# Two attention layers of a decoder: row maxima taken over two PSUM banks at once, exponentials of one head from one bank

## The chip, the core and the metric

The kernel runs on one core of one Trainium2 chip. Its time is the device time of one launch in microseconds (us). Three executions of the kernel before are shown below, with the one that was profiled beside them.

## What is computed

The program is a decoder of twelve layers over an activation of 4 batches x 1024 tokens x 256 features: quantised attention, cross attention, experts, normed attention, a small product, local attention, a state-space layer, another product, a spiking feed-forward layer, linear attention, causal attention, and a retrieval layer. After each comes a residual sum and a layer norm. The change touches two of them, whose reference is, cut to what matters (16 heads of 16 features, sequence length 1024, context length 77):

```python
# normed attention (layer 1, attn)
q = _layernorm((x @ Wq + bq).reshape(b, s, NH, HD), q_scale, q_bias)
k = _layernorm((x @ Wk + bk).reshape(b, s, NH, HD), k_scale, k_bias)
v = _layernorm((x @ Wv + bv).reshape(b, s, NH, HD), v_scale, v_bias)
scores = jnp.einsum('bqhd,bkhd->bhqk', q, k) * HD ** (-0.5)
probs = jax.nn.softmax(scores, axis=-1)
return jnp.einsum('bhqk,bkhd->bqhd', probs, v).reshape(b, s, NH * HD) @ Wo + bo

# causal attention over context and own keys (layer 3, xattn)
q = x @ Wq
k, v = jnp.split(jnp.concatenate((mem, x), axis=1) @ Wkv, 2, axis=-1)
dots = jnp.einsum('bhid,bhjd->bhij', q, k) * scale
dots = jnp.where(j_idx > i_idx + mem_len, -jnp.inf, dots)
out = jnp.einsum('bhij,bhjd->bhid', jax.nn.softmax(dots, axis=-1), v)
return out @ Wout + bout
```

## The kernel before

One function, `split_attention` (L243), builds four of the attention layers (modes "quant", "cross", "normed" and "causal"); the constants that matter are P = 128, GROUP = 512, PACK = 4 heads, HGS = 4 head groups, HALVES = 2, TILES = 8. Queries and keys are split into bf16 parts and stacked on partitions, so that one bf16 matmul gives the exact score of a head. A softmax without overflow needs each query's maximum before its exponential, so each head group is worked through twice.

The **first pass** (steps "max") makes scores with the queries on the partitions: for each of 8 query tiles of 128 and each of 4 heads, a matmul of the query tile against 512 keys into a bank of the tile `ring` (L529, with a masking matmul L532 on the causal diagonal), and a `reduce_max` on VectorE from that bank into `row_max` (L724). Normed has 64 such steps in a head group (2 halves of the keys each); causal has 48, fewer at the early query tiles, and 8 more for the 77 context keys of all four heads (L525, L719). After a group's last maximum the step "turn" reduces and negates the maxima, splits them into three bf16 parts (L728 to L734), turns them with a matmul (L537), copies them out (L739) and sends them through DRAM to the extra rows of `query_stack` (L804, L806), from where the second pass subtracts them inside its matmul.

The **second pass** works in slots. A slot is one tile of 128 keys (or the context), 512 queries (a half) and the four heads of a group. It has the steps ("scores", n, 0), ("scores", n, 1) and, one slot later, ("values", n): a scores step is two matmuls of 512 columns, one a head, into two of the four banks of the tile `scores` (L555, mask L558), and one `exp` of ScalarE over both banks into `probs` (L644); a values step is four fp32 matmuls that accumulate in `outputs` (L575). Normed has 16 slots in a group (8 tiles of keys by 2 halves). Causal has 14 (context and 4 tiles, context and 8 tiles), and those on the diagonal have 384, 256 or 128 columns to a head. After a half's last slot follow "raw" (ScalarE copies `outputs`, L652), "sums" (L583, reciprocal L749) and "normal" (ScalarE L656, matmuls L592, VectorE L753), two and four slots later.

`main_order` (L311) writes the order of the steps, and every engine walks this one list. While group g runs its second pass, the first pass of group g+1 is spread over all but the last three slots: `share` in each, cut into three pieces that stand between the two scores steps (`share[:cuts[0]]`), before the values step and after it. In the groups where queries and keys of another half of the heads are projected (`prepare`: groups 0 and 2 of a batch) the projection's steps stand in the early slots as well, two after each scores step. The last group of the last batch has no maxima beside it. At the start of each layer stands one first pass by itself (`first_order`, for group 0 of batch 0). The batches 0 to 2 are a loop, batch 3 stands alone.

What holds the engines together are counting semaphores on these PSUM tiles. The ring (steps "project", "vproj", "vars", "spread", "max", "turn", "sums", "normal") has two places: step r may be written when step r-2 has been read. The scores tile has two places of two banks: scores step e may be written when exponential e-2 is done.

```python
                            if e >= 2:
                                pe.wait_ge(scores_read if quantised else probs_ready, e - 1)
```

PSUM has 8 banks, all given out here: scores 4, ring 2, outputs 2.

## Time and profile before

| | us |
|---|---|
| median of 3 runs | 12553.13 |
| lowest and highest | 12539.91, 12562.37 |
| the profiled execution | 12566.82 |
| its span in the trace | 12564.9 |
| busy in the span: PE, DVE, ACT, POOL | 9118.7, 6511.5, 4259.1, 2322.7 |
| mean granted TensorE clock, share of 2.4 GHz | 0.818 |

PE is TensorE, PEld its weight loads, DVE VectorE, ACT ScalarE, POOL GpSimd. In a timeline row stand the start from the span's begin, the duration of all that the row merges, engine, line, operation, output<-inputs, shapes, count, and in brackets the idle time of the engine before the row and what ended it. "issue" there means that no wait which the profile shows ended it. Matmuls are pipelined: a row of one matmul lasts longer than the distance to the next. The normed layer's work on attention lies between 2902 and 4370 us, the causal layer's between 9480 and 10610 us.

### The profile page before, as it was taken

The page shows a single profiled execution, that of the slowest core. Times are in us where ns is not written, and L with a number is a line of the kernel's source. Part 1 is how long each engine was busy: PE and PEld are TensorE (multiplying, and loading weights), DVE is VectorE, ACT ScalarE, POOL GpSimd, SP SyncE. Part 2 cuts the span into 40 slices and gives each one's busy share as a digit, 9 for nine tenths or more (in the row PEclk, how much of TensorE's full clock was granted, in tenths as well). Part 3 has the DMA queues.
Part 4 walks back from the last instruction along what each step waited for, and adds up shares of the span by engine and source line. Part 5 has one row for each costly group of instructions (what it writes and reads, how often), then busy time and mean ns, then how long its engine had stood idle before and what let it go on. Part 6 is the DMA issues. An engine that isn't in the chain of part 4 may idle for free. (4 is left out here: it accounts for less than half of the span.)

```text
span 12564.9 us, 119074 instructions
## 1 busy us (share of the span) xinstructions
PE 9118.7 (73%) x41714; PEld 4719.9 (38%) x41826; DVE 6511.5 (52%) x11716; ACT 4259.1 (34%) x6517; POOL 2322.7 (18%) x1916
## 2 busy tenths in 40 slices
PE   4777574975888889888957667677886887454555
PEld 1222243542333356456422222233443443343344
DVE  6666332015556556256258878855344554444443
ACT  3555221112444446255133333322112433232222
POOL 1000002011101011011013323310001000455555
PEclk8888665986999989999978778788777998777777
DMA  3210111112111000000000000000002221568677
GB/s 62 38 32 16 33 31 60 66 57 39 26 22 31 17 11 2 8 11 9 0 11 0 0 0 0 0 9 2 3 0 44 41 32 24 134 142 153 139 148 155
DMA packets 228075, 505.07 MB, mean 40 GB/s; under 512 B 46859, under 2 KB 87669, under 8 KB 226071
## 3 DMA queue, kind: packets, MB, share of 16 engines
q0 software_dynamic: 88064, 282.15, 10.3%
q1 hardware_dynamic: 139527, 216.73, 8.6%
q8 instruction: 273, 4.47, 0.2%
q14 instruction: 211, 1.73, 0.0%
HBM read 426.36 MB, written 75.53 MB: 40 GB/s over the span
## 5 line engine op out<-in xcount | busy, mean ns | idle before, releaser
L644 ACT ACTIVATE probs<-scores 128x1024 f32<-128x1024 f32 (+4 forms) x1024 | 927.4, 941 | 1270.0 <-PE scores L555 974.1
L724 DVE TENSOR_REDUCE row_max<-ring 128x1 f32<-128x512 f32 (+3 forms) x1792 | 1046.5, 628 | 351.0 <-PE ring L529 274.3
L2715 POOL DMA_INDIRECT r_got<-in_L_ffn_tables,r_pick_now x1024 | 988.1, 965 | 674.4 <-issue 288.8
L2803 PE MATMUL r_psum_y<-r_diagonal,r_got 128*128 128x128 f32 x4096 | 611.7, 317 | 522.5 <-ACT r_diagonal L2850 343.2
L555 PE MATMUL scores<-query_stack,key_stack 99*128 99x512 bf16 (+3 forms) x2816 | 856.9, 398 | 140.6 <-DVE levels L746 57.4
L2636 DVE TENSOR_TENSOR_SCAN state<-decay,added 128x1024 f32<-128x1024 f32 x256 | 871.0, 3402 | 35.6 <-ACT decay L2611 31.5
L575 PE MATMUL outputs<-probs,head_values 128*32 128x512 f32 (+3 forms) x5632 | 765.2, 617 | 106.1 <-ACT probs L641 104.2
L2803 PEld LDWEIGHTS r_psum_y<-r_diagonal,r_got 128*128 128x128 f32 x4096 | 589.0, 231 | 579.2 <-ACT r_diagonal L2850 379.7
L529 PE MATMUL ring<-key_stack,query_stack 96*128 96x512 bf16 (+3 forms) x1792 | 642.8, 388 | 151.6 <-DVE row_max L724 59.8
L641 ACT ACTIVATE probs<-levels,quant 128x1024 f32<-128x1024 uint8 x512 | 610.9, 1233 | 388.0 <-DVE levels L746 386.5
L2619 POOL TENSOR_TENSOR added<-ssm_du,state_in_rows 128x1024 f32<-128x1024 f32 x256 | 608.4, 2377 | 592.4 <-DVE state L2636 576.4
L746 DVE TENSOR_SCALAR levels<-scores 128x1024 uint8<-128x1024 f32 x512 | 606.0, 1219 | 135.4 <-PE scores L555 111.3
L2587 PE MATMUL state_sums<-term,constants 128*128 128x512 f32 x1024 | 638.9, 759 | 8.1 <-DVE ssm_u L2627 8.1
L2611 ACT ACTIVATE decay<-ssm_dt,a_log 128x1024 f32<-128x1024 f32 x256 | 294.1, 1149 | 647.5 <-DVE state L2636 647.5
L555 PEld LDWEIGHTS scores<-query_stack,key_stack 99*128 99x128 bf16 x2816 | 261.3, 106 | 624.0 <-DVE levels L746 278.7
L167 ACT ACTIVATE norm_squares<-norm_sum 128x512 f32<-128x512 f32 x208 | 127.6, 630 | 1047.2 <-DVE norm_sum L192 1035.8
L2938 DVE CUSTOM_DVE_ANT_0 r_scratch<-r_got,r_rows_now 128x256 f32<-128x256 f32 x1024 | 378.9, 421 | 191.2 <-DMA r_got<-in_L_ffn_tables,r_pick_now 108.0
L2198 POOL TENSOR_TENSOR norm_squares<-qk,rope 128x256 f32<-128x256 f32 x256 | 180.9, 739 | 1594.0 <-DVE qk L2122 1594.0
L529 PEld LDWEIGHTS ring<-key_stack,query_stack 96*128 96x128 bf16 x1792 | 164.0, 100 | 738.3 <-DVE row_max L724 519.2
L490 PE MATMUL ring<-norm_sum,split_w 128*128 128x512 f32 x448 | 273.4, 755 | 219.8 <-DVE norm_sum L220 128.0
L1929 PE MATMUL window_products<-wide_w,shifted 128*128 128x512 f32 x768 | 365.2, 627 | 57.9 <-DVE shifted L2099 49.3
L2572 PE MATMUL state_out<-ssm_states,pick 96*128 96x512 bf16 x512 | 169.6, 416 | 309.2 <-DVE term L2641 308.3
(512 smaller groups left out, 16197.9 us busy)
## 6 DMA issues: line engine op xcount, KB each, us to landing
expert_w<-in_L_ffn_w SPq DMA_DIRECT2D x16, 1024.0 KB, 10.4
r_got<-in_L_ffn_tables,r_pick_now POOLq DMA_INDIRECT x1024
quant_parts<-parts SPq DMA_DIRECT2D x48, 256.0 KB, 5.5
query_stack<-quant_parts SPq DMA_DIRECT2D x48, 256.0 KB, 8.3
key_stack<-quant_parts SPq DMA_DIRECT2D x48, 256.0 KB, 8.7
query_stack<-cross_parts SPq DMA_DIRECT2D x48, 256.0 KB, 8.2
normed_parts<-parts SPq DMA_DIRECT2D x48, 256.0 KB, 4.9
query_stack<-normed_parts SPq DMA_DIRECT2D x48, 256.0 KB, 8.4
```

The costliest lines, as they stand in the source:

```text
L529: last = nc.tensor.matmul(out[:, 0:cols], lhs, k_stack[0:max_row, h, j * GROUP:j * GROUP + cols], start=True, stop=not edge)
L555: last = nc.tensor.matmul(out[:, off:GROUP], keys, q_stack[0:rows, h, half * GROUP + off:(half + 1) * GROUP], start=True, stop=not edge)
L575: last = nc.tensor.matmul(o_ps[SLOT * i:SLOT * (i + 1), half, off:GROUP], vals, probs[0:k_rows, n % 2, i // 2, i % 2, off:GROUP], start=fi ...
L641: nc.scalar.activation(dst, levels[:, e % 2, :, :], ACT.Exp, bias=quant[:, 4:5], scale=scale).then_inc(probs_ready, 1)
L644: nc.scalar.activation(dst, s_ps[0:k_rows, 2 * (e % 2):2 * (e % 2) + 2, off:GROUP], ACT.Exp, scale=scale).then_inc(probs_ready, 1)
L724: nc.vector.reduce_max(row_max[:, i, qt, at:at + 1], src[:, 0:cols], AX.X).then_inc(ring_read, 1)
L746: ts(levels[:, e % 2, :, :], s_ps[:, 2 * (e % 2):2 * (e % 2) + 2, :], 0.0, QMAX, ALU.max, ALU.min).then_inc(scores_read, 1)
L2587: last = nc.tensor.matmul(sum_ps[:, half(j)], chip.c(C_ID), term[:, i % 2, half(j)], start=(n == 0), stop=(n == STATES - 1))
L2619: nc.gpsimd.tensor_tensor(added[:, i % 2, :], du[:, i // STATES, :], state_in[:, i % 2, :], ALU.mult).then_inc(added_ready, 1)
L2636: nc.vector.tensor_tensor_scan(state[:, i % 2, :], decay[:, i % 2, :], added[:, i % 2, :], 0.0, ALU.mult, ALU.add).then_inc(state_ready, 1)
L2715: nc.gpsimd.indirect_dma_start(out=b["got"][:, n, :], out_offset=None, in_=b["tables"], in_offset=bass.IndirectOffsetOnAxis(ap=b["pick_now ...
L2803: last = nc.tensor.matmul(y_ps[:, c, t * P:(t + 1) * P], row, b["diagonal"][:, k % 2, n, :], start=False, stop=(k == RHEADS * per - 1 and ...
```

## The change

In the modes normed and causal a maximum step now covers all keys of a query tile: one or two matmuls into the two banks of one ring place, and one `reduce_max` over up to 1024 elements. The ring has still two places, now of two banks each (4 banks). The scores tile has two banks, each a place for one head: after each score matmul stands its own semaphore step, and ScalarE does one exponential for each head from one bank. Modes quant and cross are as before. Core of the diff:

```diff
@@ -260,7 +260,9 @@
     blocks = [(t, m) for m in range(2) for t in range(sides)]
-    kinds = (1 if context else 0) + (HALVES if own else 0)
+    kinds = (1 if context else 0) + (1 if own else 0)
+    score_heads = 1 if maxed and own else 2
+    ring_banks = 2 if maxed and own else 1
 
...
@@ -282,7 +284,7 @@
             if own:
-                out += [(qt, i, j) for i in range(PACK) for j in range(1 + qt // PER_HALF if causal else HALVES)]
+                out += [(qt, i, (qt + 1) * P if causal else SEQ) for i in range(PACK)]
         return out
...
@@ -513,10 +515,11 @@
                         elif kind == "max":
-                            _, g, nx, qt, i, j = step_
+                            _, g, nx, qt, i, cols = step_
                             if step_[3:] == first_pass(g)[0]:
                                 stacks_ready(g, nx)
                             out = ring_bank(step_)
+                            both = r_ps[:, ring[step_] % 2, :, :].rearrange("p j t -> p (j t)")
                             heads = range(PACK) if i is None else [i]
...
@@ -524,12 +527,12 @@
                                 else:
-                                    cols = min(GROUP, (qt + 1) * P - j * GROUP) if causal else GROUP
-                                    edge = causal and j == qt // PER_HALF
-                                    last = nc.tensor.matmul(out[:, 0:cols], lhs, k_stack[0:max_row, h, j * GROUP:j * GROUP + cols],
-                                                            start=True, stop=not edge)
-                                    if edge:
-                                        last = nc.tensor.matmul(out[:, cols - P:cols], chip.id_bf[:, :], chip.far_n[:, :], start=False, stop=True)
+                                    for at in range(0, cols, GROUP):
+                                        end = min(at + GROUP, cols)
+                                        edge = causal and end == cols
+                                        last = nc.tensor.matmul(both[:, at:end], lhs, k_stack[0:max_row, h, at:end], start=True, stop=not edge)
+                                        if edge:
+                                            last = nc.tensor.matmul(both[:, cols - P:cols], chip.id_bf[:, :], chip.far_n[:, :], start=False, stop=True)
                             last.then_inc(ring_ready, 1)
...
@@ -539,30 +542,31 @@
                             g, half, kt, off = slots[n]
-                            e = 2 * n + pair
                             if n % per_group == 0 and pair == 0:
                                 stacks_ready(g, 0)
                                 if ("turn", g, 0) in turns:
                                     pe.wait_ge(top_loaded, 16 * (turns[("turn", g, 0)] + 1))
-                            if e >= 2:
-                                pe.wait_ge(scores_read if quantised else probs_ready, e - 1)
                             for i in range(2):
+                                e = (4 * n + 2 * pair + i) // score_heads
+                                if e >= 2 and i % score_heads == 0:
+                                    pe.wait_ge(scores_read if quantised else probs_ready, e - 1)
                                 h = PACK * g + 2 * pair + i
                                 k_rows = CTX if kt is None else P
                                 keys = keys_now[0:rows, h, :] if kt is None else k_stack[0:rows, h, kt * P:(kt + 1) * P]
-                                out = s_ps[0:k_rows, 2 * (e % 2) + i, :]
+                                out = s_ps[0:k_rows, score_heads * (e % 2) + i % score_heads, :]
                                 edge = diagonal(half, kt)
                                 last = nc.tensor.matmul(out[:, off:GROUP], keys, q_stack[0:rows, h, half * GROUP + off:(half + 1) * GROUP],
                                                         start=True, stop=not edge)
                                 if edge:
                                     last = nc.tensor.matmul(out[:, off:off + P], chip.id_bf[:, :], chip.far_t[:, :], start=False, stop=True)
-                            last.then_inc(scores_ready, 1)
+                                if i % score_heads == score_heads - 1:
+                                    last.then_inc(scores_ready, 1)
                         elif kind == "values":
                             n = step_[1]
                             g, half, kt, off = slots[n]
                             k_rows = CTX if kt is None else P
                             first, final = (kt, off) == items(half)[0], (kt, off) == items(half)[-1]
-                            pe.wait_ge(probs_ready, 2 * n + 2)
+                            pe.wait_ge(probs_ready, PACK // score_heads * (n + 1))
                             if own and n == old_slots:
...
@@ -631,18 +635,21 @@
                             g, half, kt, off = slots[n]
-                            e = 2 * n + pair
                             k_rows = CTX if kt is None else P
                             if n >= 2:
                                 act.wait_ge(outputs_added, n - 1)
                             dst = probs[0:k_rows, n % 2, pair, :, off:GROUP]
                             if quantised:
+                                e = 2 * n + pair
                                 act.wait_ge(scores_read, e + 1)
                                 nc.scalar.activation(dst, levels[:, e % 2, :, :], ACT.Exp, bias=quant[:, 4:5], scale=scale).then_inc(probs_ready, 1)
                             else:
-                                act.wait_ge(scores_ready, e + 1)
-                                nc.scalar.activation(dst, s_ps[0:k_rows, 2 * (e % 2):2 * (e % 2) + 2, off:GROUP], ACT.Exp,
-                                                     scale=scale).then_inc(probs_ready, 1)
+                                for i in range(0, 2, score_heads):
+                                    e = (4 * n + 2 * pair + i) // score_heads
+                                    bank = score_heads * (e % 2)
+                                    act.wait_ge(scores_ready, e + 1)
+                                    nc.scalar.activation(dst[:, i:i + score_heads, :], s_ps[0:k_rows, bank:bank + score_heads, off:GROUP], ACT.Exp,
+                                                         scale=scale).then_inc(probs_ready, 1)
                         elif kind == "raw":
...
@@ -714,14 +721,13 @@
                         elif kind == "max":
-                            _, g, nx, qt, i, j = step_
+                            _, g, nx, qt, i, cols = step_
                             if i is None:
                                 nc.vector.reduce_max(row_max[:, :, qt, 0], src[:, 0:PACK * CTX].rearrange("p (i n) -> p i n", i=PACK),
                                                      AX.X).then_inc(ring_read, 1)
                             else:
-                                cols = min(GROUP, (qt + 1) * P - j * GROUP) if causal else GROUP
-                                at = j + kinds - HALVES
-                                nc.vector.reduce_max(row_max[:, i, qt, at:at + 1], src[:, 0:cols], AX.X).then_inc(ring_read, 1)
+                                both = r_ps[:, r % 2, :, :].rearrange("p j t -> p (j t)")
+                                nc.vector.reduce_max(row_max[:, i, qt, kinds - 1:kinds], both[:, 0:cols], AX.X).then_inc(ring_read, 1)
                         elif kind == "turn":
...
@@ -813,7 +819,7 @@
         def batch(order, b, b_next):
-            with banks(nc, "scores", [P, 4, GROUP], F32) as s_ps, banks(nc, "ring", [P, 2, GROUP], F32) as r_ps, \
+            with banks(nc, "scores", [P, 2 * score_heads, GROUP], F32) as s_ps, banks(nc, "ring", [P, 2, ring_banks, GROUP], F32) as r_ps, \
                     banks(nc, "outputs", [P, 2, GROUP], F32) as o_ps:
                 attend(order, b, b_next, s_ps, r_ps, o_ps)
             if b is not None:

```

The hunks left out give the new counts to the other waits (`PACK // score_heads * old_slots` on `scores_ready`, and `r_ps[:, r % 2, 0, :]` for the ring steps of one bank).

What it does to the order of instructions, at two places. TensorE, normed layer, two slots of a group with maxima, before (L529 is a maximum's matmul, L555 a score's, L575 a value's):

```order
L555 MATMUL scores<-query_stack,key_stack 128x512 x2
L529 MATMUL ring<-key_stack,query_stack 128x512
L555 MATMUL scores<-query_stack,key_stack 128x512 x2
L529 MATMUL ring<-key_stack,query_stack 128x512 x2
L575 MATMUL outputs<-probs,head_values 32x512 x4
L529 MATMUL ring<-key_stack,query_stack 128x512 x2
L555 MATMUL scores<-query_stack,key_stack 128x512 x2
L529 MATMUL ring<-key_stack,query_stack 128x512
L555 MATMUL scores<-query_stack,key_stack 128x512 x2
L529 MATMUL ring<-key_stack,query_stack 128x512 x2
L575 MATMUL outputs<-probs,head_values 32x512 x4
L529 MATMUL ring<-key_stack,query_stack 128x512 x2
```

and the same place of the changed kernel (L533, L558 and L579 are those lines now):

```order
L558 MATMUL scores<-query_stack,key_stack 128x512 x4
L533 MATMUL ring<-key_stack,query_stack 128x512 x2
L579 MATMUL outputs<-probs,head_values 32x512 x4
L533 MATMUL ring<-key_stack,query_stack 128x512 x4
L558 MATMUL scores<-query_stack,key_stack 128x512 x4
L533 MATMUL ring<-key_stack,query_stack 128x512 x2
L579 MATMUL outputs<-probs,head_values 32x512 x4
L533 MATMUL ring<-key_stack,query_stack 128x512 x2
```

Between the first and the second pair of score matmuls stood one maximum; now all four score matmuls of a slot follow each other, since `len(share) // 5` is 0 for shares of two, three or four. A maximum is a row of x2 now: the first slot shown has one before its values and two behind them, the second has one and one.

ScalarE, normed layer, from the first slots after the projections on, before (L644 is the exponential):

```order
L644 ACTIVATE probs<-scores 128x1024 x8
L652 ACTIVATE raw_out<-outputs 128x512
L644 ACTIVATE probs<-scores 128x1024 x6
L656 ACTIVATE wide_inverse<-inverse 128x512
L644 ACTIVATE probs<-scores 128x1024 x10
L652 ACTIVATE raw_out<-outputs 128x512
L644 ACTIVATE probs<-scores 128x1024 x6
```

and now (L651):

```order
L651 ACTIVATE probs<-scores 128x512 x16
L659 ACTIVATE raw_out<-outputs 128x512
L651 ACTIVATE probs<-scores 128x512 x12
L663 ACTIVATE wide_inverse<-inverse 128x512
L651 ACTIVATE probs<-scores 128x512 x20
L659 ACTIVATE raw_out<-outputs 128x512
L651 ACTIVATE probs<-scores 128x512 x12
```

Each exponential became two of half the size; nothing else moved on ScalarE.

In slots without maxima TensorE's rows read alike before and now (four score matmuls, four values matmuls). What differs there is that the third and the fourth score matmul now wait for the exponentials of the first and the second head of their own slot, where before they waited for the slot before.

## Rows read from the trace of the kernel before

**Rows 1.** Page, part 5: shapes, count, busy us, mean ns, idle us.

```profile
L644 ACT ACTIVATE probs<-scores 128x1024 f32<-128x1024 f32 (+4 forms) x1024 | 927.4, 941 | 1270.0 <-PE scores L555 974.1
L724 DVE TENSOR_REDUCE row_max<-ring 128x1 f32<-128x512 f32 (+3 forms) x1792 | 1046.5, 628 | 351.0 <-PE ring L529 274.3
```

**Rows 2.** Stretches of the normed stage, first line naming the columns.

```profile
core 0: us, PE busy (x) PEld busy (x) DVE busy (x) ACT busy (x) POOL busy (x), PEclk, DMA share, GB/s
2970.00:3015.00 45.00, 37.74 (x63) 6.44 (x63) 39.94 (x62) 0.00 (x0) 0.00 (x0) 0.50 0.00 0
3290.00:3590.00 300.00, 249.92 (x1236) 100.45 (x1228) 174.28 (x295) 131.96 (x143) 23.81 (x14) 0.92 0.10 17
4290.00:4335.00 45.00, 40.76 (x254) 10.96 (x246) 1.89 (x4) 36.66 (x41) 0.00 (x0) 1.00 0.01 2
```

**Rows 3.** Timeline, one normed slot with maxima: start us, us, instruction.

```profile
3446.65 3.11 DVE L724 TENSOR_REDUCE row_max<-ring 128x1 f32<-128x512 f32 x5 [0.57 <-PE ring L529]
3446.66 0.60 PE L555 MATMUL scores<-query_stack,key_stack 99*128 99x512 bf16 x2
3447.36 1.98 ACT L644 ACTIVATE probs<-scores 128x1024 f32<-128x1024 f32 x2 [0.40 <-PE scores L555]
...
3447.39 0.39 PE L529 MATMUL ring<-key_stack,query_stack 96*128 96x512 bf16 x1
...
3448.91 1.06 PE L575 MATMUL outputs<-probs,head_values 128*32 128x512 f32 x8
```

**Rows 4.** ScalarE's timeline, normed: where a group with maxima begins and ends.

```profile
3116.08 1.94 ACT L644 ACTIVATE probs<-scores 128x1024 f32<-128x1024 f32 x2 [1.97 <-PE scores L555]
...
3177.22 1.94 ACT L644 ACTIVATE probs<-scores 128x1024 f32<-128x1024 f32 x2 [0.38 <-PE scores L555]
```

**Rows 5.** Timeline, normed, the last batch's last group, without maxima.

```profile
4293.60 1.94 ACT L644 ACTIVATE probs<-scores 128x1024 f32<-128x1024 f32 x2 [0.33 <-PE scores L555]
...
4313.14 0.11 PEld L555 LDWEIGHTS scores<-query_stack,key_stack 99*128 99x128 bf16 x2 [0.32 <-ACT probs L644]
...
4313.68 1.06 PE L575 MATMUL outputs<-probs,head_values 128*32 128x512 f32 x8
...
4314.68 1.34 PE L555 MATMUL scores<-query_stack,key_stack 99*128 99x512 bf16 x4
...
4316.94 1.06 PE L583 MATMUL ring<-constants,raw_out 128*128 128x4 f32 x8
...
4334.09 0.60 ACT L652 ACTIVATE raw_out<-outputs 128x512 f32<-128x512 f32 x1 [1.19 <-PE outputs L575]
```

**Rows 6.** Groups by shape, causal stage, 9540 to 10590 us.

```profile
L724 DVE TENSOR_REDUCE row_max<-ring 128x1 f32<-128x512 f32 x384 | 255.3, 687 | 67.5 <-PE ring L529 46.7 <-PE ring L532 12.9
...
L644 ACT ACTIVATE probs<-scores 128x512 f32<-128x512 f32 x64 | 36.4, 596 | 91.4 <-PE scores L558 91.4
```

**Rows 7.** Groups by shape, normed stage, 2960 to 4340 us.

```profile
L652 ACT ACTIVATE raw_out<-outputs 128x512 f32<-128x512 f32 x32 | 19.1, 598 | 17.0 <-PE outputs L575 17.0
...
L699 DVE TENSOR_REDUCE value_root<-norm_squares 128x64 f32<-128x1024 f32 x7 | 8.5, 1210 | 0.0
```

**Rows 8.** Timeline, normed, after a group's last maximum.

```profile
3107.76 0.22 DVE L728 TENSOR_REDUCE top<-row_max 128x32 f32<-128x64 f32 x1
...
3109.44 0.23 PE L537 MATMUL ring<-identity_bf,top_parts 128*96 128x128 bf16 x1 [0.96 <-DVE top_parts L731]
...
3115.38 1.04 PE L555 MATMUL scores<-query_stack,key_stack 99*128 99x512 bf16 x4 [1.58 <-DMA query_stack<-normed_top]
```

**Rows 9.** ScalarE's timeline, causal: a group with maxima, and the last one.

```profile
9654.48 1.93 ACT L644 ACTIVATE probs<-scores 77x1024 f32<-77x1024 f32 x2 [2.31 <-PE scores L555]
...
9706.97 1.93 ACT L644 ACTIVATE probs<-scores 77x1024 f32<-77x1024 f32 x2 [3.54 <-PE scores L555]
...
10552.24 1.93 ACT L644 ACTIVATE probs<-scores 77x1024 f32<-77x1024 f32 x2 [2.27 <-PE scores L555]
...
10584.62 0.66 ACT L644 ACTIVATE probs<-scores 128x256 f32<-128x256 f32 x2 [0.37 <-PE scores L558]
```

10 lines of the change are left out of this document (5 added, 5 removed).

## The prediction

> **What bounds the kernel now.** I read the page's groups first, then the stretches of the two layers, then single slots in the timeline. The page's groups [rows 1] give the two instructions that the change merges and splits: 1792 reductions of VectorE with a mean of 628 ns and 1024 exponentials of ScalarE with a mean of 941 ns. Of these 1024 the change leaves 64 of cross attention alone. No engine is full in these layers: in 300 us of the normed layer [rows 2] PE is busy 250 us by a count that overstates it, DVE 174, ACT 132. So the time is made by hand-offs between engines, and one slot has to be read in the timeline.
>
> In a slot with maxima [rows 3] DVE works 3.11 us on five reductions and idles 0.57 us, so such a slot lasts 3.68 us. PE has four score matmuls, five of maxima and four values matmuls. A row of two 512-column matmuls lasts 0.60 us where one alone lasts 0.39, so they follow each other at 0.21; nine make 1.9 us. The values matmuls hold PE for 1.00 us, from 4313.68 to the next score matmul at 4314.68 [rows 5]. That is 3.0 us of PE in 3.68. The rest is mostly PE waiting for a place in the ring. ACT, with two exponentials in 1.98 us, idles for the rest. A whole group of 16 slots lasts 61.1 us, 3116.08 to 3177.22 [rows 4].
>
> Three hand-off times come from the same rows. Score matmul to exponential: the pair starts at 3446.66, its second matmul 0.21 later, the exponential at 3447.36, so 0.48 from a matmul's start to its reader's. Reader to matmul: the first reduction starts at 3446.65 and lasts 0.68, the matmul it lets go starts at 3447.39, so 0.06. Last score matmul to the values: 4313.14 plus 0.21 to 4313.68 [rows 5], 0.32.
>
> **VectorE's part.** 512 pairs of reductions in the normed layer and 256 in the causal one (query tiles 4 to 7 of 4 groups, 4 heads, 4 batches) become one each. A reduction of 512 elements takes 687 ns from PSUM [rows 6]; one of 1024 takes 1210 ns from SBUF [rows 7]. None of 1024 from two banks is in this trace: it lies between 1210 and 2 x 687 = 1374 ns. I take 1210, since only the source differs. Five reductions follow each other at (3.11 - 0.68) / 4 = 0.61 us, so a merged one follows at about 1.15: a pair saves 0.07 to 0.16 us of DVE. Where DVE alone sets the pace this is the whole gain. The first pass that stands alone is such a place: 62 reductions in 45 us with the clock at 0.50 [rows 2], some 0.70 each with the hand-off. 64 of them are 44.8 us, 32 merged ones at 1.23 are 39.4: 5 us less, and 2 less in the causal layer.
>
> A rule of the Trainium skill speaks here. "VectorE: DVE Perf Modes", in its section on the TRN2 errata, gives 120 cycles at 0.96 GHz as fixed for a PSUM source, paid once for each instruction. By that a merged pair saves 0.125 us, and if DVE's instruction cost decided everywhere the 768 pairs would give 96 us. The trace agrees with the size but not with the use: DVE idles 0.57 us in each slot [rows 3].
>
> **ScalarE's part, and the wait it adds.** 960 exponentials become 1920. One of 512 elements (two heads of 256) takes 596 ns [rows 6]; a copy of one full bank takes 598 [rows 7], so I take 0.60 for one head and 0.50 from start to start (two of 1.02 take 1.94 to 1.98, so they overlap by about 0.1). ACT has room for that. What counts is the place for the result. Before, scores place e waited for exponential e-2, which was a pair of the slot before, long done. Now it is a head of the same slot, so the third score matmul waits for the first head's exponential and the fourth for the second's. From the first exponential's start of a full slot: the second starts at 0.50 and ends at 1.10, the fourth matmul starts at 1.16, the values 0.32 later at 1.48, they hold PE to 2.48, and the next slot's first exponential starts 0.48 after that, at 2.96. Behind the waiting matmul everything of PE is queued: values, maxima, sums.
>
> The bounds of this slot: 2.48 if the second exponential's end cost nothing (0.48 shorter), 3.2 if a hand-off costs twice what it does here. I take 2.96, because each piece has a row. The slot without maxima lasts 2.12 us before: from 4293.60 to 4334.09 a group lasts 40.5 us [rows 5], of which the sums and normals of two halves take some 6.
>
> *Normed, last group of the last batch.* 16 x 2.96 + 5 for sums, normals and raw copies is 52.5 against 40.5: **+12**.
>
> *Normed, groups with maxima and no projection.* A maximum is two matmuls, 0.43 us of PE, 32 of them in a group. 16 x 2.96 = 47.4; 13.8 for maxima; two sums and two normals at some 0.9 each (eight passes in 1.06 [rows 5]) 3.7; the turn 1.0, since its chain of 1.7 us on DVE (3107.76 to 3109.44 [rows 8]) starts a reduction later; 0.3 for a raw copy. Sum 66.2, against 61.1 [rows 4]. Ring places come in time: with three maxima to a slot DVE has 3.5 us of work in 4.2, and the place of each is read before PE needs it. Eight such groups: 8 x 5.0 = **+40**. The transfer of the maxima (5.9 us from the turn to the next group's first matmul [rows 8]) now lies under two longer slots and costs nothing more.
>
> *Normed, groups with projections.* Seven groups. In slots 1 to 6 the projection's steps stand between the two score pairs and cover the wait, and DVE's saving counts there, some 0.3 a slot. The ten other slots lose as above, less what sums and normals win when DVE is not the one waited for: some +3. Together +1.4 each, **+10**.
>
> *Causal.* A group lasts 52.5 us, 9654.48 to 9706.97 [rows 9]; the others of this kind average 51.5. Eight of 14 slots are full ones at 2.96 (3.05 for the masked ones); 384, 256 and 128 columns give 2.5, 1.9 and 1.6 by the same sum. That is 35.7 for the group. Maxima take 12 of PE, sums and normals 3.7, the turn 1.4, the transfer behind it 1.3 (two narrow last slots do not cover 5.9), and about 1 goes to places in the ring, where four wide maxima stand in one slot. Sum 55: +3.5, eight times, **+28**. With projections I take +2.5, seven times, **+17**. The last group (32.4 us, 10552.24 to 10584.62 [rows 9]) goes to 39.5, **+7**.
>
> *Sum.* Normed 12 + 40 + 10 - 5 = +57, causal 28 + 17 + 7 - 2 = +50, together +107 us. The profiled execution, 12566.8, becomes 12674. It lies 13.7 above the median of the runs, so against that median I predict **12660**. Quant and cross attention keep their code and their time. SP and POOL queues keep their steps; their waits on scores come at the same slot.
>
> **Rivals.** A difference within 0.2%, 25 us, is about what a measurement cannot tell from none.
>
> *DVE sets the pace (faster, 0.14).* PE waits for ring places in every slot with maxima before, and if the new wait for ACT falls wholly into that old one, a slot goes with DVE: 2.46 reductions at 1.15 plus the old 0.57 of idleness is 3.40, against 3.68. With 13 such slots in 15 groups that is -55, half as much in the causal layer, -7 for the first passes, and +19 for the last groups: about -70, **12480**. For it: DVE is what PE is seen waiting for [rows 1]. Against: four scores without a maximum between them put 0.7 us of waiting where PE has nothing else. The point from which it decides is that wait: under about 0.35 us a slot the kernel is faster.
>
> *The two cancel (0.11).* If the ring's stalls in the groups with projections and in the causal layer shrink by 3 us more in each group than I count, 22 groups give back 66, and the time is 12590 or less, down to 12560.
>
> *The clock falls (slower, 0.15).* The lone first pass, where PE waits in every step, was granted 0.50 (1.2 GHz), the last group, where PE hardly waits, 1.00 (2.4 GHz) [rows 2]. If the slots without maxima, PE working 1.9 us in 2.96, or others fall to 1.2 GHz, such a slot takes matmuls of 0.43 and values of 2.0 and lasts some 4.4. A slot with maxima gains about 3. The layers have 256 + 224 = 480 slots; one in twenty at half clock is +72, one in ten +144, on top of the forecast: **12730** to 12800. "TensorE: Matmul & The Clock Gate", Part 1, says that the throttled state is the default and that activity releases it. This rule speaks against the change, which thins PE's work. Against this rival: slots at 3.0 in 3.68 us run at 0.92.
>
> **How the numbers follow.** Forecast 0.60 (12600 to 12740, from 2 us less to 2.5 more in each of 30 groups), the rivals 0.14, 0.11 and 0.15. Slower is 0.60 + 0.15 = 0.75, same 0.11, faster 0.14. The range leaves out half of the faster case and the clock's far end: 12530 to 12770; the forecast's own is 12600 to 12740.
>
> **What would show it.** Exponentials of one head at 0.60 and reductions at 1.2 us. Normed slots without maxima at 2.96 and with them at 3.8 and 4.2. PE's score matmuls waiting for the exponential, some 0.7 us a slot, where they hardly waited before, and PE's waits for `row_max` mostly gone. A normed group of 66 us. I would be wrong if score matmuls three and four start without a wait, if full slots with maxima stay below 3.7, or if the granted clock falls clearly.

## The result, and the profile after

The change makes the kernel slower.

| | before | after |
|---|---|---|
| median of 4 runs, us | 12557.75 | 12754.08 |
| lowest and highest | 12539.91, 12592.83 | 12750.59, 12759.7 |
| ratio, 95% interval | | 1.0153 [1.0131, 1.0176] |
| span in the trace | 12564.9 | 12748.8 |
| busy: PE, DVE, ACT | 9118.7, 6511.5, 4259.1 | 9201.2, 6455.6, 4357.7 |

That is +196 us between the medians and +184 between the traces, where +107 was predicted. The lines below are those of part 5 of the page of after that answer to [rows 1], with the score matmuls beside them (L558 for L555).

```profile
L651 ACT ACTIVATE probs<-scores 128x512 f32<-128x512 f32 (+5 forms) x1984 | 1023.8, 566 | 1338.2 <-PE scores L558 970.5
L730 DVE TENSOR_REDUCE row_max<-ring 128x1 f32<-128x1024 f32 (+7 forms) x1024 | 986.2, 988 | 568.2 <-PE ring L533 347.3
L558 PE MATMUL scores<-query_stack,key_stack 99*128 99x512 bf16 (+3 forms) x2816 | 944.0, 405 | 355.1 <-ACT probs L651 200.7
```

VectorE has 60 us less to do in its maxima (1046.5 to 986.2) and idles 217 more before them; ScalarE has 96 us more in its exponentials. TensorE's line is the one to read: 201 us of its score matmuls' idle time end with an exponential. The view of waits says it for both halves of the engine (columns: us in total, times, longest). Before:

```profile
PEld ring L529 <- DVE row_max L724: 519.2, 878, 1.7
...
PE ring L529 <- DVE row_max L724: 59.8, 226, 1.3
PEld scores L555 <- ACT probs L644: 57.1, 85, 1.6
```

After:

```profile
PEld scores L558 <- ACT probs L651: 601.3, 887, 2.6
PE scores L558 <- ACT probs L651: 217.5, 438, 2.1
...
PEld ring L533 <- DVE row_max L730: 173.9, 244, 1.7
```

The wait for a ring place (579 us by these two lines before, 195 after) has given way to a wait for the exponential (57 before, 819 after). PEld and PE overlap, so these are no parts of the time, but the exchange is plain.

One normed slot without maxima, of the last group, in the timeline of after (it answers to [rows 5]):

```profile
4369.45 2.22 ACT L651 ACTIVATE probs<-scores 128x512 f32<-128x512 f32 x4 [0.72 <-PE scores L558]
4370.09 0.10 PEld L558 LDWEIGHTS scores<-query_stack,key_stack 99*128 99x128 bf16 x1 [1.02 <-ACT probs L651]
4370.10 0.88 PE L558 MATMUL scores<-query_stack,key_stack 99*128 99x512 bf16 x2 [0.53 <-ACT probs L651]
4370.58 0.10 PEld L558 LDWEIGHTS scores<-query_stack,key_stack 99*128 99x128 bf16 x1 [0.39 <-ACT probs L651]
4370.90 0.16 PEld L579 LDWEIGHTS outputs<-probs,head_values 128*32 128x32 f32 x8 [0.23 <-issue]
4370.91 1.06 PE L579 MATMUL outputs<-probs,head_values 128*32 128x512 f32 x8
```

The third score matmul starts 0.65 after the first exponential's start, the fourth 0.48 later, the values at 1.46. The prediction had 1.16 for the fourth and 1.48 for the values.

Where the time went is read from the starts of each group's first exponential. Normed, a group with maxima (it answers to [rows 4]; the last slots before its end stand too):

```profile
3120.57 2.22 ACT L651 ACTIVATE probs<-scores 128x512 f32<-128x512 f32 x4 [0.72 <-PE scores L558]
...
3180.17 2.22 ACT L651 ACTIVATE probs<-scores 128x512 f32<-128x512 f32 x4 [1.65 <-PE scores L558]
3183.12 2.22 ACT L651 ACTIVATE probs<-scores 128x512 f32<-128x512 f32 x4 [0.72 <-PE scores L558]
3186.06 2.22 ACT L651 ACTIVATE probs<-scores 128x512 f32<-128x512 f32 x4 [0.72 <-PE scores L558]
```

65.5 us, where it was 61.1. Causal, a group with maxima (it answers to [rows 9]), with its five slots from the first full one of the second half on, between 10025.03 and 10053.30:

```profile
10003.26 2.23 ACT L651 ACTIVATE probs<-scores 77x512 f32<-77x512 f32 x4 [0.83 <-PE scores L558]
...
10025.03 2.22 ACT L651 ACTIVATE probs<-scores 128x512 f32<-128x512 f32 x4 [0.41 <-PE scores L558]
10031.24 1.09 ACT L651 ACTIVATE probs<-scores 128x512 f32<-128x512 f32 x2 [3.99 <-PE scores L558]
10032.59 1.09 ACT L651 ACTIVATE probs<-scores 128x512 f32<-128x512 f32 x2 [0.27 <-PE scores L558]
10037.73 2.22 ACT L651 ACTIVATE probs<-scores 128x512 f32<-128x512 f32 x4 [4.05 <-PE scores L558]
...
10042.94 2.22 ACT L651 ACTIVATE probs<-scores 128x512 f32<-128x512 f32 x4 [2.47 <-PE scores L558]
10047.78 2.28 ACT L651 ACTIVATE probs<-scores 128x512 f32<-128x512 f32 x4 [2.62 <-PE scores L561]
10053.30 0.87 ACT L651 ACTIVATE probs<-scores 128x384 f32<-128x384 f32 x2 [3.23 <-PE scores L561]
...
10062.25 2.23 ACT L651 ACTIVATE probs<-scores 77x512 f32<-77x512 f32 x4 [2.21 <-PE scores L558]
```

59.0 us for the group, and 28.3 for the five slots. The same group of before lasts from 9917.27 to 9969.60, 52.3 us, and its five slots 22.3:

```profile
9939.18 1.94 ACT L644 ACTIVATE probs<-scores 128x1024 f32<-128x1024 f32 x2 [0.62 <-PE scores L555]
...
9961.52 1.51 ACT L644 ACTIVATE probs<-scores 128x768 f32<-128x768 f32 x2 [2.66 <-PE scores L558]
```

By kind of group, each length being the distance between two such starts (the last group: to its last exponential) and the first pass counted from its first reduction to the first exponential, the layers split so. "Seven" are the groups with projections, "eight" the others with maxima.

| us | first pass | seven | eight | last | sum |
|---|---|---|---|---|---|
| normed, before | 52.9 | 653.5 | 615.3 | 38.3 | 1360.0 |
| normed, after | 46.2 | 651.3 | 653.0 | 51.8 | 1402.3 |
| normed, predicted change | -5 | +10 | +40 | +12 | +57 |
| normed, measured | -7 | -2 | +38 | +14 | **+42** |
| causal, before | 44.3 | 439.4 | 521.9 | 32.7 | 1038.3 |
| causal, after | 40.3 | 492.9 | 594.4 | 45.7 | 1173.3 |
| causal, predicted change | -2 | +17 | +28 | +7 | +50 |
| causal, measured | -4 | +54 | +73 | +13 | **+135** |

42 and 135 make 177 of the 184 us between the traces. The normed layer did what was forecast; the causal one lost almost three times as much. The stretches of the causal layer, from its first exponential to its last, show the clock (columns as in [rows 2]). Before:

```profile
9590.00:10586.00 996.00, 870.03 (x5991) 412.36 (x5989) 531.91 (x1106) 421.77 (x543) 90.34 (x63) 0.93 0.22 36
```

After, and below it the slot that begins at 10031.24:

```profile
9633.00:10766.00 1133.00, 950.01 (x5973) 415.62 (x5974) 505.34 (x866) 466.00 (x989) 90.28 (x62) 0.89 0.19 31
...
10030.00:10037.00 7.00, 6.68 (x30) 2.26 (x30) 2.19 (x5) 2.17 (x4) 0.00 (x0) 0.53 0.00 0
```

Since the granted clock has two levels, 1.2 and 2.4 GHz, a stretch of L us granted c has spent 2 (1 - c) L at the lower one: some 139 us before and 249 after, each uncertain by about 11 through the rounding of c. The normed layer was granted 0.92 before (3024.9 to 4332) and 0.93 after (3028.2 to 4384): there this time did not grow.

### The profile page after: what moved, and what is told of

The parts are those of the page before. It is cut to its first block and busy times, and to the rows that moved or that the text cites. A ratio compares the mean times of both kernels' runs of the same rounds, so it can differ in the third digit from the quotient of the medians.

```text
span 12748.8 us, 119266 instructions
## 1 busy us (share of the span) xinstructions
PE 9201.2 (72%) x41714; PEld 4712.1 (37%) x41826; DVE 6455.6 (51%) x10948; ACT 4357.7 (34%) x7477; POOL 2321.7 (18%) x1916
## 5 line engine op out<-in xcount | busy, mean ns | idle before, releaser
L651 ACT ACTIVATE probs<-scores 128x512 f32<-128x512 f32 (+5 forms) x1984 | 1023.8, 566 | 1338.2 <-PE scores L558 970.5
L730 DVE TENSOR_REDUCE row_max<-ring 128x1 f32<-128x1024 f32 (+7 forms) x1024 | 986.2, 988 | 568.2 <-PE ring L533 347.3
L558 PE MATMUL scores<-query_stack,key_stack 99*128 99x512 bf16 (+3 forms) x2816 | 944.0, 405 | 355.1 <-ACT probs L651 200.7
L579 PE MATMUL outputs<-probs,head_values 128*32 128x512 f32 (+3 forms) x5632 | 779.7, 629 | 104.9 <-ACT probs L645 104.5
L558 PEld LDWEIGHTS scores<-query_stack,key_stack 99*128 99x128 bf16 x2816 | 262.2, 105 | 1068.1 <-ACT probs L651 555.6
L533 PE MATMUL ring<-key_stack,query_stack 96*128 96x512 bf16 (+3 forms) x1792 | 541.9, 389 | 75.6 <-DMA key_stack<-normed_parts 36.7
L2259 PE MATMUL gated_psum<-norm_sum,gated_w 128*128 128x512 f32 x768 | 347.1, 615 | 6.9 <-DVE norm_sum L2306 6.9
```

Of the source, the lines that this page charges most:

```text
L533: last = nc.tensor.matmul(both[:, at:end], lhs, k_stack[0:max_row, h, at:end], start=True, stop=not edge)
L558: last = nc.tensor.matmul(out[:, off:GROUP], keys, q_stack[0:rows, h, half * GROUP + off:(half + 1) * GROUP], start=True, stop=not edge)
L579: last = nc.tensor.matmul(o_ps[SLOT * i:SLOT * (i + 1), half, off:GROUP], vals, probs[0:k_rows, n % 2, i // 2, i % 2, off:GROUP], start=fi ...
L651: nc.scalar.activation(dst[:, i:i + score_heads, :], s_ps[0:k_rows, bank:bank + score_heads, off:GROUP], ACT.Exp, scale=scale).then_inc(pr ...
L730: nc.vector.reduce_max(row_max[:, i, qt, kinds - 1:kinds], both[:, 0:cols], AX.X).then_inc(ring_read, 1)
```

## The experiments

The kernel before was measured anew beside each group of runs. Its median is 12562.25 us beside the first four runs below, 12337.34 beside the next four, 12343.78 beside balanced, warm and three_job_balanced, and 12354.67 beside balanced_warm. So each ratio stands against the before that was measured beside it, and medians in us are not to be compared across these groups. The 200 us between them lie behind the two layers: from the causal layer's last exponential to the end of the trace it is 1980 to 2011 us in before, after and the first four runs, and 1768 to 1780 in the others; why is not known. The layers' own times can be compared over all runs: code that was equal gave 1305.9 and 1307.0 us for the normed layer of before and 1348.2 to 1356.0 for that of after (first exponential to last, as all layer times below). The layers' differences add up to 5 to 35 us less than those of the medians. Repeats of equal code in the causal layer lie up to 9 us apart, and less than that is read as nothing here.

### One layer at a time

The function of before stands beside that of after, and one of the two layers calls it:

```diff
-        split_attention(chip, "causal", params)
+        split_attention_old(chip, "causal", params)
```

(normed_only; causal_only does it for "normed".)

> The change in the normed layer alone, the causal layer as before. In the two traces the normed layer's first pass went from 52.9 to 46.2 us and its main part from 1307 to 1356, so +42 us over before if the layers are independent: about 12600. If part of the loss lies elsewhere (other layers, another clock state), it would be over +60 or under +25.

Measured: 12622.0, ratio 1.0044 [1.003, 1.0059]; normed 1348.2 (before 1307.0), causal 985.4 (994.0). That is 60 us between the medians for the 42 expected, at the edge of what the expectation allowed; the normed layer itself, with its first pass, is 35 us longer.

> The change in the causal layer alone. Traces: first pass 44.2 to 40.3 us, main part 994 to 1133, so +135 us, about 12690. The hand-off sum of the prediction gave +50 for it. The rival (what is missing is not the causal layer's own, but a chance of the profiled execution's clock) expects +50 to +80.

Measured: 12715.38, ratio 1.0124 [1.0108, 1.0141]; normed 1305.9, causal 1128.8, near the expectation. The two excesses, 0.44% and 1.24%, add up to 1.68% against the 1.53% of the whole change: within the intervals the layers do not touch each other, and most of the loss is the causal layer's.

### The exponentials alone, with two places and with four

Both keep the maxima and the ring of before and give each head its exponential. One has two places of one bank for scores, as the change has; the other four, which is all of the four banks that before uses.

```diff
+    score_heads = 1 if maxed and own else 2
+    places = 2 if maxed and own else 2
...
                             for i in range(2):
+                                e = (4 * n + 2 * pair + i) // score_heads
+                                if e >= places and i % score_heads == 0:
+                                    pe.wait_ge(scores_read if quantised else probs_ready, e - places + 1)
```

(exp_only_4: `places = 4 if maxed and own else 2`.)

> Exponentials of one head, two places of one bank, maxima as before (ring of two single banks). Place theory: PE has the waits of the changed kernel and in addition the old waits for ring places, with DVE's work per slot at 3.1 us instead of 2.8: the same as the changed kernel or up to 120 us slower, 12750 to 12870. If the merged maxima are what costs, this is close to before, under 12620.

Measured: 12738.76, ratio 1.0138 [1.0121, 1.0155]; normed 1381.9, causal 1082.6.

> As the last, but with four places of one bank (the four banks that the scores had before). Place theory: the fourth matmul again waits only for a head of the slot before, so the time is that of before within 40 us, though ScalarE does 1920 exponentials instead of 960. Instruction theory (the count of exponentials and of their semaphore steps costs): about as slow as the changed kernel, over 12680.

Measured: 12567.77, ratio 1.0004 [0.999, 1.0018]; normed 1309.5, causal 989.4. This pair is the core of the study: the first came out just under its expectation (12750 or more), the second as expected. The same 1984 exponentials, in the pages' part 5, first with two places:

```profile
L650 ACT ACTIVATE probs<-scores 128x512 f32<-128x512 f32 (+5 forms) x1984 | 1025.5, 567 | 1309.3 <-PE scores L557 963.2
...
L557 PE MATMUL scores<-query_stack,key_stack 99*128 99x512 bf16 (+3 forms) x2816 | 931.8, 400 | 266.0 <-ACT probs L650 110.5
```

and with four:

```profile
L650 ACT ACTIVATE probs<-scores 128x512 f32<-128x512 f32 (+5 forms) x1984 | 982.3, 574 | 1195.2 <-PE scores L557 917.6
...
L557 PE MATMUL scores<-query_stack,key_stack 99*128 99x512 bf16 (+3 forms) x2816 | 849.2, 396 | 138.1 <-DVE levels L752 55.2
```

The view of waits shows the mechanism itself. TensorE's waits for an exponential, with two places:

```profile
PEld scores L557 <- ACT probs L650: 454.5, 870, 2.1
...
PE scores L557 <- ACT probs L650: 116.7, 285, 1.4
```

and with four, where they are back at the 57 us of before:

```profile
PEld scores L557 <- ACT probs L650: 49.9, 95, 0.8
```

960 more instructions on ScalarE cost nothing that can be measured; what costs is that two heads of scores can be under way and not four. Halving the places alone (exp_only_2 against exp_only_4) makes +72 us in the normed layer and +93 in the causal one; against before it is +75 and +89. Merging the maxima as well (after against exp_only_2) gives back 26 us in the normed layer (and 7 in its first pass), and costs 50 more in the causal one (1133.0 against 1082.6). Single groups say the same: the second group of each batch lasts in the causal layer 51.5 us on average before, 57.0 with two places, 59.7 after; the five slots above last 22.3, 25.2 (10030.60 to 10055.80) and 28.3. So the causal loss has two parts, the places and the merging, and the second is looked at further below.

### Three places

The changed kernel with a third place for scores. Its bank comes from `outputs`, which gets one bank; the first values matmul of a half then waits for the raw copy of the half before.

```diff
+    places, out_banks = (3, 1) if maxed and own else (2, 2)
...
-                                if e >= 2 and i % score_heads == 0:
-                                    pe.wait_ge(scores_read if quantised else probs_ready, e - 1)
+                                if e >= places and i % score_heads == 0:
+                                    pe.wait_ge(scores_read if quantised else probs_ready, e - places + 1)
...
-                            if first and g:
-                                pe.wait_ge(raw_ready, HALVES * (g - 1) + half + 1)
+                            made = HALVES * g + half
+                            if first and made >= out_banks:
+                                pe.wait_ge(raw_ready, made - out_banks + 1)
```

> The changed kernel with a third scores place, its bank taken from outputs (one bank instead of two, each half's first values waits for the copy of the half before). Place theory: the third matmul waits for nothing, the fourth for the first head; a full slot without maxima goes from 2.96 to about 2.46 us, 0.5 us a slot over 480 slots: some -200 us from the changed kernel, 12550 or below. Clock theory (the causal layer's loss is the clock): in the causal layer alone more than half of the gain. Instruction theory: no gain, 12750.

Measured: 12380.09, ratio 1.0037 [1.0024, 1.005]; normed 1277.1, which is 30 us below before, causal 1052.4. By the ratios that is some 145 us less than after, where 200 were expected. ScalarE's timeline in the last normed group:

```profile
4255.79 2.07 ACT L653 ACTIVATE probs<-scores 128x512 f32<-128x512 f32 x4 [0.39 <-PE scores L559]
4258.25 2.06 ACT L653 ACTIVATE probs<-scores 128x512 f32<-128x512 f32 x4 [0.39 <-PE scores L559]
```

A slot is 2.46 us with three places, 2.94 with two: 0.48 less, and near the 2.48 that the prediction had as the lower bound of a slot. One bank moved takes back about three quarters of the loss, and turns the normed layer's sign: with the wait shortened, it is faster than before. That this is the gain of the merged maxima is likely but not shown, for no run has three places without them.

### Work between the score matmuls

Two ways to fill the wait without a bank. In the first the values step of the slot before stands between the two pairs of score matmuls, and the second piece of the slot's maxima with it (values_between; values_before is the same move in the kernel before, as a control). In the second one maximum of each slot does (job_between).

```diff
+            early = own and maxed
...
-            order.append(("scores", n, 1))
-            order += maxima(target, nx, share[cuts[0]:cuts[1]])
+            if not early:
+                order.append(("scores", n, 1))
+                order += maxima(target, nx, share[cuts[0]:cuts[1]])
             if n:
...
+            if early:
+                order += maxima(target, nx, share[cuts[0]:cuts[1]])
+                order.append(("scores", n, 1))
```

```diff
-            cuts = [len(share) // 5, 3 * len(share) // 5]
+            cuts = [min(1, len(share)) if own and maxed else len(share) // 5, max(1, 3 * len(share) // 5)]
```

> The changed kernel with the values step moved between the two score pairs, so that PE has 1.0 us of work where it waits for exponentials. Place theory: a full slot without maxima 2.96 to 2.67 us, with maxima PE is free of the wait and DVE's 2.8 us decides, 4.0 to about 3.2: -200 to -350 us, 12400 to 12550, below before. If the waits are not what costs, nothing changes (12750).

Measured: 12405.1, ratio 1.0051 [1.0035, 1.0068]; normed 1311.4, causal 1050.3. By the ratios some 125 us less than after; 200 to 350 were expected, and a time below before.

> The same move in the kernel before. PE hardly waits for exponentials there, DVE's 3.1 us a slot stays: -50 to +30 us, so 12510 to 12590. If the move by itself is worth as much as in the changed kernel (rival: it smooths the ring's use), -150 or more.

Measured: 12420.77, ratio 1.0059 [1.0043, 1.0076]; normed 1353.2, causal 1005.5. That is +83 us, where -50 to +30 were expected. The move slows the kernel before, which has the wait hardly at all: it is no gain in itself. Most of the loss sits in the normed groups with maxima alone (615.3 to 642.5 us) and in the last one (38.3 to 53.0).

> The changed kernel with one maximum of every slot moved between the score pairs. It fills 0.43 us of the wait of some 0.7: 0.4 us in 13 of 16 normed and 11 of 14 causal slots of 15 groups each, 360 x 0.4 = -140 us from the changed kernel, about 12610. If the wait is not filled by it, or the ring stalls in its place, under -50.

Measured: 12414.98, ratio 1.0065 [1.0049, 1.0082]; normed 1311.5, causal 1066.0. By the ratios some 110 us less than after, where 140 were expected. Against the spans of the unchanged code given above (1348.2 to 1356.0, and 1128.8 to 1133.0) both moves give back 37 to 45 us in the normed layer and 63 to 83 in the causal one. The waits tell the same: TensorE's waits for an exponential, 819 us in after, are 287 in values_between and 474 in job_between, where the waits for a ring place grew from 195 to 416. Two different fillers gain where this wait shrinks, which supports that the wait itself is what is paid for.

### The late causal slots: the share, and the clock

What makes the second half of the causal miss? `main_order` deals out the maxima of a group by count, over 11 slots. Before there were 56 of them, none wider than 512; now there are 40, and the 16 that cover over 512 columns, two matmuls and a masking matmul each, all belong to the late query tiles and fall into the late slots. Where the time lies is read from the starts of the exponentials, added up over the fifteen causal groups with maxima. "Late" are the five slots marked out above, "first" the six before them, "end" the last three slots with the way to the next group:

| us | first | late | end | last group | sum |
|---|---|---|---|---|---|
| before | 417 | 319 | 225 | 33 | 994 |
| exp_only_2 | 446 | 363 | 229 | 45 | 1083 |
| after | 433 | 416 | 238 | 46 | 1133 |
| balanced (below) | 448 | 376 | 244 | 46 | 1114 |

The late slots alone make 97 of the layer's 139 us, and the whole of what merging adds (53 for 50, the other parts nearly cancel). One late slot of after in the timeline:

```profile
10028.53 0.11 PEld L533 LDWEIGHTS ring<-key_stack,query_stack 96*128 96x128 bf16 x2
10028.54 0.45 PE L533 MATMUL ring<-key_stack,query_stack 96*128 96x512 bf16 x2
10028.69 1.56 DVE L730 TENSOR_REDUCE row_max<-ring 128x1 f32<-128x640 f32 x2 [0.21 <-PE ring L535]
...
10029.57 1.13 PE L587 MATMUL ring<-constants,raw_out 128*128 128x4 f32 x8 [0.52 <-DVE row_max L730]
...
10030.55 1.02 PE L558 MATMUL scores<-query_stack,key_stack 99*128 99x512 bf16 x2
...
10031.89 1.10 PE L558 MATMUL scores<-query_stack,key_stack 99*128 99x512 bf16 x2 [0.32 <-ACT probs L651]
...
10033.92 1.93 PE L579 MATMUL outputs<-probs,head_values 128*32 128x512 f32 x8
```

The sums at 10029.57 wait 0.52 us for a ring place behind two wide reductions. From about 10030.4 on the matmuls run at the lower clock level (a row of two 1.02 where it was 0.60, the values 1.93 where they were 1.06), and the slot whose first exponential starts at 10031.24 lasts 6.49 us, to 10037.73. TensorE had waited several times in the microseconds before that: for this ring place, and for the exponentials of its own slot. Three runs try to separate the share and the clock. `balanced` deals by columns, a maximum over 512 counting twice; `warm` puts a spare matmul, overwritten by the one behind it, ahead of the second score matmul of a slot; `balanced_warm` has both.

```diff
+            if causal and jobs:
+                weights = [2 if job[2] and job[2] > GROUP else 1 for job in jobs]
+                starts = [sum(weights[:k]) for k in range(len(jobs))]
+                share = [job for job, at in zip(jobs, starts) if s < spread and sum(weights) * s // spread <= at < sum(weights) * (s + 1) // spread]
```

```diff
+                                if causal and i and not pair:
+                                    nc.tensor.matmul(out[:, 0:GROUP], keys, q_stack[0:rows, h, half * GROUP:(half + 1) * GROUP], start=True, stop=True)
```

> The changed kernel; in the causal layer alone a slot's share of maxima is counted in keys' halves (a merged maximum of over 512 keys counts two) instead of in steps, so that the wide ones do not all fall into the last five slots of the share. The causal layer's main part was 1133 us in the changed kernel, 1083 with the same exponentials and unmerged maxima. Share theory: the 50 us between are the uneven share, so 1085 to 1100, and the ratio to before falls from 1.015 to about 1.012. Rival (the two-bank reduction itself, or the ring's coarser places, cost them): within 15 us of 1133.

Measured: 12503.37, ratio 1.0141 [1.0119, 1.0162]; causal 1113.9, granted 0.89 as in after. Expected were 1085 to 1100 if the share were all of the 50 us, and within 15 of 1133 if it were nothing; it lies between.

> The changed kernel; in the causal layer every slot's second score matmul is preceded by a spare matmul of 512 columns into the same place, overwritten by the real one, in a stretch where TensorE waits for an exponential anyway (slack 0.29 us in a full slot, spare 0.22; narrow slots pay some 0.1 to 0.2, 6 of 14, +12 us in the layer). Clock theory: part of the causal layer's loss is the granted clock, which in the changed kernel is 1.2 GHz for 76 us in slot 7 of the groups, against 18 before: the low-clock time of the layer falls from 239 us to under 190 and the main part from 1133 to 1110 or below. Rival (low clock there costs nothing, since other engines are waited for): the low-clock time falls, the time rises by 0 to 15 us.

Measured: 12508.93, ratio 1.0135 [1.0118, 1.0152]; causal 1117.9, granted 0.91, so some 201 us at the lower level. Both went the expected way and less far (under 190 us and 1110 or below were expected).

> Both last single changes in the changed kernel: the causal share counted in halves of keys, and the spare matmul where TensorE waits. Each alone took 19 and 15 us from the causal layer's main part (1133). If share and clock are two separate causes: 1095 to 1105, low-clock time under 200 us, close to the 1083 of the kernel with unmerged maxima, and what is left of the 50 us would be the ring's coarser places. If the two act on the same slots (the low clock of slot 7 is itself made by the share): 1110 to 1118.

Measured: 12505.86, ratio 1.0124 [1.0107, 1.0142]; causal 1103.2, granted 0.91; 1095 to 1105 was expected for two separate causes. The ratios' intervals overlap that of after, so the reading rests on the layer's own time: 1133.0 and 1128.8 for the unchanged code, 15 to 19 us less with the even share, 11 to 15 less with the spare matmuls, 26 to 30 less with both. The even share left the granted clock where it was and took 40 us out of the late slots, of which 15 came back in the first slots and 6 at the end: this part is shown. The spare matmuls' gain lies only just above the 9 us by which equal code differs, and it is spread evenly (5 us in the first slots, 5 in the late ones, 4 at the end), so it is indicated and no more. That the two gains add up in the third run speaks for two separate causes. Together they account for about half of the 50 us that merging costs in this layer; the other 20 to 25 stay open. After the even share what is left against exp_only_2 lies in the late slots (13 us) and at the groups' ends (15).

### All that helped, together

Three places, one maximum between the pairs and the even share:

> Three places for scores (one bank of outputs), one maximum of each slot between the score pairs, and the share of the causal maxima counted in halves of keys. Sums from the single runs: normed main part 1277 (three places), less 0.43 in 13 of 16 slots of eight groups and less in the others, about 1225; causal 1052, less 30 for the share and 20 for the job between, about 1000; first passes 11 us shorter than before. Against before 1307 and 994: -80 us, ratio 0.993. If DVE decides normed slots at 3.2 us (its work is 2.8), normed stays at 1250: ratio 0.996.

Measured: 12299.75 against 12343.78 for before, ratio 0.9961 [0.9946, 0.9975]; normed 1267.0, causal 986.0. It is the one version that is faster than before, if only by 0.4% where 0.7% was expected: -40 us in the normed layer, -6 and -4 in the first passes, and the causal layer level with before (-8, within the 9 us of equal code). The causal layer in it:

```profile
9520.50:10506.50 986.00, 872.52 (x5974) 413.68 (x5976) 506.98 (x866) 451.57 (x989) 90.28 (x62) 0.91 0.22 36
```

against the same window of balanced_warm, with two places:

```profile
9623.60:10726.80 1103.20, 973.07 (x6201) 433.13 (x6203) 510.41 (x866) 475.61 (x989) 90.31 (x62) 0.91 0.20 32
```

The granted clock is the same, the length is not: here the places and the filled wait decide, not the clock.

## Why the prediction was right in kind and too small in size

**VectorE's part: right.** A reduction over 1024 columns of two banks takes 1222 ns (482 of them in the normed layer), for the 1210 taken, so a pair costs 2 x 687 - 1222 = 152 ns less; the first passes became 7 and 4 us shorter, for 5 and 2. "VectorE: DVE Perf Modes" in the Trainium skill, section on the TRN2 errata, gives 120 cycles, 0.125 us, as fixed for each instruction with a PSUM source; the measured saving is somewhat larger. As the prediction held against the rule, it buys nothing by itself: merging gave back 26 us in the normed layer and cost 50 in the causal one. (62 reductions in 45 us [rows 2] are 0.73 us each and not "some 0.70"; the first pass's gain is a difference and hardly moves by it.)

**ScalarE's part: right.** One head takes 595 ns, for 0.60. A full slot without maxima lasts 2.94 us, for 2.96. The chain "third matmul waits for the first head's exponential" is in the rows, and exp_only_4 shows that the exponentials cost nothing besides it: with four places the loss is gone.

**Normed: right, with one term too large.** Slots with two and three maxima at 3.81 and 4.24, for 3.8 and 4.2; a group at 65.5, for 66.2; the eight groups +38, for +40; the last +14, for +12. The +38 is in part luck: five of the eight lost 5.8 us each, for 5.0, and the three that lead over to the next batch only 2.9. The seven with projections came out at -2 and not +10: their steps seem to cover more of the wait than counted, which no run shows by itself. Together +42 for +57.

**Causal: the mechanism right, the size not, and this is the step that failed.** The prediction added up a group as "35.7" for slots, "12" for maxima and "about 1 ... to places in the ring, where four wide maxima stand in one slot", and came to +3.5 a group and +2.5 with projections. Measured are +9.1 (73 / 8: five groups +8.1, the three that lead over to the next batch +10.7) and +7.6 (54 / 7). Three things were missed:

- Places alone cost +5.6 in the eight groups, +4.5 in the seven and +12 in the last one (exp_only_2), not 3.5, 2.5 and 7. A likely reason, which no run tests, is that the sum took slots and maxima as if each slot had its average of maxima.
- Merging was taken as a gain for VectorE everywhere. It also changes what `main_order` deals out: steps of equal count, no longer of equal length. The prediction's own sentence on four wide maxima in one slot saw this and priced it at 1 us; the late slots grew by 53 us when the maxima were merged, 3.5 a group. The even share takes 40 of them out, but only 15 to 19 us of the layer remain as gain, a little over 1 us a group.
- The clock. What the prediction kept as a rival, and named as a sign of being wrong, came partly true, in this layer alone. It spends about 110 us more at 1.2 GHz (139 to 249). A slot without maxima lasts 4.25 us at that level (10744.20 to 10748.46 and 4328.18 to 4332.43; 4.4 was estimated) and 2.94 at the other, so some 31% of that time is loss: an estimate, for slots with maxima were not measured at both levels, of about 34 us of the 139 that the layer lost (994.0 to 1133.0). The spare matmuls took away some 48 us at the lower level (249 to 201, each uncertain by about 11) and gave back 11 to 15, near the 31% of 48.

The last causal group shows it as well, +13 for +7:

```profile
10720.00:10766.00 46.00, 39.35 (x224) 13.70 (x225) 1.89 (x4) 26.54 (x59) 0.00 (x0) 0.81 0.00 1
...
4332.00:4384.00 52.00, 41.56 (x216) 10.95 (x214) 1.89 (x4) 35.99 (x67) 0.00 (x0) 0.95 0.00 1
```

It was granted 0.81 and the normed one 0.95, where the normed one had 1.00 before [rows 2].

**The rivals.** That VectorE sets the pace falls: it idles more than before, not less. But three_places shows how near that case was: with the wait shortened by the 0.48 us of one hand-off the normed layer becomes faster than before by 30 us. The prediction had 0.7 us of waiting a slot and put the turning point at 0.35; 0.48 less leaves 0.2, which is past it, and there the layer is indeed faster. That the two cancel falls too: the time moved by 1.5%. The clock's rival described a part of the causal layer, and its price, 12730 and up, is where the time came out; but it is not the main cause: exp_only_2 has a causal layer granted 0.91 (9651.6 to 10734.2), so 56 us more at the lower level than before, some 17 of its 89 us; and balanced_warm, granted 0.91 too, is still 109 us above before in that layer.

The median, 12754.08, is 94 us over the predicted 12660 and inside the range to 12770, but above the forecast's own range to 12740. About 15 us too much in the normed layer stand against 85 too little in the causal one, which is 70; 19 us lie between the difference of the medians and that of the two layers, and 5 in the median of before, which its fourth run raised. The way and the cause were forecast. That the time still lies in the stated range is partly luck: the range reaches to 12770 only for the sake of the clock's rival, and an error in the normed layer offset a part of the causal one.

## What to carry to other kernels

When PSUM banks are dealt anew between stages, count for each stage the results that can be under way, not its instructions: here 960 more exponentials were free, and two places fewer for their inputs cost more than 160 us. Merging steps also changes whatever is dealt out by their number, so deal by length (19 us of a layer of 1133 here). Where a place can't be had, independent work between the write and the wait takes back a good part (0.9% and 1.0% of the 1.5% lost), and a single third place took back at least as much as either reordering.

## What the runs showed of the hardware

- A VectorE maximum over 1024 columns reads across two PSUM banks in one instruction at 1222 ns, where one over 512 takes 687 [rows 6]: 0.15 us less for a pair.
- The granted clock fell to 0.89 in the causal layer and held at 0.93 in the normed one, though both got waits of the same kind in each slot. What tells the two apart is left open; the spare matmuls show only that with more work of TensorE between the waits the causal layer was granted 0.91.
- The move of the values step cost the kernel before 0.6%, and its eight normed groups without projections 27 us (615.3 to 642.5); why was not followed further.
